# Value products of groups 3, 6, 9 and 12 in two parts, one of them with VectorE's subtraction; output products moved

## The chip, the cores and the metric

One core of a Trainium2 chip runs the whole program. The metric is the time of one execution in microseconds (us); lower is better. The five engines run their own instruction queues in order and meet at semaphores: PE (TensorE), DVE (VectorE), ACT (ScalarE), POOL (GpSimd) and SP, which here only issues DMAs.

## The reference, cut to what matters

```
x = x + xattn(layernorm(x), ctx)     # 256 rows, 16 heads of 128, 4 key/value heads, 4096 context rows
x = x + mamba2(layernorm(x))
x = x + experts(layernorm(x))        # 32 experts, top 6, and a shared one

scores = einsum('blhd,bmhd->bhlm', q, k_full) * scale + mask     # m: 4096 context rows and 256 own rows
probs  = softmax(scores, axis=-1)
out    = einsum('bhlm,bmhd->blhd', probs, v_full)
return out.reshape(B, L, nh * hd) @ wo
```

Everything is in float32. The change is in the cross attention and in the hand-over from it to the second part.

## The kernel before

The program is written out by hand, one function for each engine; the order of the calls in it is the order on the engine. About 240 us go to projecting the context, 450 us to the attention, 60 us to the second part and 230 us to the experts.

In the attention the 4352 keys of a head are 17 groups of 256 (`NG`); group 16 (`SELF`) holds the own rows and a causal mask. A counter `s` runs over the 272 groups in which scores are made, and `n = s - LEAD` (29 groups behind) over the groups whose weights meet the values. So one step of TensorE, `in_turns(score(s), weigh(n), n)`, interleaves six score matmuls for a later head with the value products of group n. All engines' loops run over the same steps:

- ScalarE copies the scores out of PSUM (`take_scores(s)`, line 1643), takes the exponential of two groups at once (`exponential`, line 1647, a "quad"), and for some groups rounds the weights to a high part (`high_of_weights`, line 1653).
- VectorE keeps the running maximum of the scores (`running_max`, lines 1093 to 1109), folds it, and subtracts the head's maximum from a quad (`subtract_max`, line 1135).
- GpSimd adds the weights of the 17 groups (`add_weights`, line 1939) and makes the low parts (`rest_of_weights`, line 1953).

A value product of a plain group is one float32 matmul for each of its two key tiles (line 641; the trace shows it as two MATMUL records). In the groups of `SPLITS` = (2, 7, 12) it is three float32r matmuls for each tile: values times high part, values times low part, low part of the values times high part (lines 635, 637, 639). The high and low parts of the weights lie in a ring of two buffers, `pT`. The low part of group n is issued on GpSimd in step n-1, the high part on ScalarE in step n-4.

The score banks are four PSUM banks in turn, so scores of group s need the maximum of group s-4 to be taken. The first head's subtractions stand `SOONER` = 4 steps ahead of the others'. `TURN_AT`, `REDUCE_AT` and `SPREAD_AT` say at which step the maxima are transposed (line 660), reduced (line 1127) and spread (line 668) for head 0, head 1, the middle heads and head 15. `sum_weights(h)` (line 675) sums a head's weights over the partitions.

The output projection needs `wo` in a high part (`wo_hi`, four loads of 1 MB, line 2155) and a low part. `project_main(0, i)` puts two float32r matmuls with the high part into step `WO_MAIN + i` = 246 + i. After the attention SP loads `w_z` for the second part, and ScalarE and VectorE split `w_xa`.

## Time and profile before

| | |
|---|---|
| median of 3 executions | 987.16 us (986.3 to 987.94) |
| profiled execution, its own time | 985.39 us |
| its span | 983.7 us |
| PE busy | 971.0 us, 99% |
| DVE busy | 769.7 us, 78% |
| ACT busy | 613.4 us, 62% |
| POOL busy | 573.8 us, 58% |
| mean granted TensorE clock | 0.998 of 2.4 GHz |

Busy shares are means over stages that differ; what a stage waits for is read in its own stretch. A busy PE may be working at half its clock.

### The profile page before, as it was taken

Reading aid. Unit: us, or ns where it says so; the run is one execution under the profiler, and the core shown is the slowest. Engines: PE = TensorE matmul, PEld = TensorE weight load, DVE = VectorE, ACT = ScalarE, POOL = GpSimd, SP = SyncE. Lnnn points to the kernel's source line nnn. Section 1 sums busy time; section 2 is a strip of 40 time slices with the busy share of each in tenths; the row PEclk is TensorE's granted clock in tenths of the full one; section 3 lists DMA queues with packets and bytes.
Section 4 is the critical chain, followed back from the end, with each engine's and each line's share of the span. In section 5 each row is a group of like instructions: output and inputs, shape, how many; then the busy total and the mean of one; then the engine's idle time right before and its main releaser. Section 6 shows DMA issues by size and latency. Waiting matters only on the chain.

```text
span 983.7 us, 15941 instructions
## 1 busy us (share of the span) xinstructions
PE 971.0 (99%) x5695; PEld 856.4 (87%) x5695; DVE 769.7 (78%) x1167; ACT 613.4 (62%) x1042; POOL 573.8 (58%) x545
## 2 busy tenths in 40 slices
PE   9999999999989999999999999989999999999998
PEld 7888888888889999999999999978789988888887
DVE  6754777654988888888898898877798877777775
ACT  5444354336757777777767767753597666666663
POOL 4754555453389999999999999993001132222222
PEclk9999999999999999999999999999999999999999
DMA  8679866679403121141105033261700785555540
GB/s 303 192 247 318 270 208 222 193 243 312 163 1 128 56 76 34 44 140 55 54 1 159 25 112 111 76 211 57 288 12 1 287 299 197 190 180 184 188 157 22
DMA packets 70926, 147.89 MB, mean 150 GB/s; under 512 B 5792, under 2 KB 50240, under 8 KB 69312
## 3 DMA queue, kind: packets, MB, share of 16 engines
q1 hardware_dynamic: 70848, 146.88, 44.1%
q8 instruction: 46, 0.75, 0.3%
q14 instruction: 32, 0.26, 0.1%
HBM read 109.60 MB, written 37.26 MB: 149 GB/s over the span
## 4 chain that ended last, share of the span: by engine, by line
PE 85%; DVE 9%; POOL 2%; DMA 1%; issue 1%; ACT 0%; SPq 0%; DVEq 0%
PE bank L641 19%; PE bank L612 17%; PE bank L520 11%; PE bank L538 11%; PE bank L941 9%; PE bank L943 5%; PE bank L749 1%; PE bank L692 1%; POOL k_rs L1908 1%; PE bank L635 1%; PE bank L637 1%; PE bank L639 1%; PE bank L547 1%; DVE turned L1071 1%; DVE bank L1109 1%
## 5 line engine op out<-in xcount | busy, mean ns | idle before, releaser
L612 PE MATMUL bank<-qT_hi,kT 128*128 128x256 f32 (+1 forms) x1088 | 295.1, 345 | 2.5 <-DVE first_max L1105 2.5
L1939 POOL TENSOR_TENSOR first_max<-first_max,weights 128x512 f32<-128x512 f32 x210 | 270.7, 1289 | 20.0
L641 PE MATMUL bank<-weights,vN 128*128 128x256 f32 (+1 forms) x896 | 259.6, 377 | 0.4 <-ACT weights L1647 0.4
L1643 ACT COPY weights<-bank 128x512 f32<-128x512 f32 (+1 forms) x272 | 154.6, 581 | 102.8 <-PE bank L612 63.4
L612 PEld LDWEIGHTS bank<-qT_hi,kT 128*128 128x128 f32 x1088 | 196.1, 189 | 21.1 <-issue 2.9
L1109 DVE TENSOR_TENSOR first_max<-bank,first_max 128x512 f32<-128x512 f32 x196 | 135.0, 689 | 34.6 <-ACT weights L1643 29.1
L1135 DVE TENSOR_TENSOR weights<-weights,bank 128x1024 f32<-128x1024 f32 x128 | 154.6, 1211 | 6.2 <-PE bank L668 6.2
L612 PE MATMUL bank<-qT_lo,kT 128*128 128x256 f32 (+1 forms) x544 | 153.5, 282 | 0.0
L1647 ACT ACTIVATE weights<-weights 128x1024 f32<-128x1024 f32 x144 | 144.0, 1003 | 9.5 <-DVE weights L1135 8.7
L641 PEld LDWEIGHTS bank<-weights,vN 128*128 128x128 f32 x896 | 142.0, 189 | 3.8 <-ACT weights L1647 0.6
L538 PE MATMUL bank<-w_ctx_hi,ctx_hl 128*128 128x512 f32 x512 | 144.4, 394 | 0.6 <-ACT w_ctx_hi L1604 0.6
L941 PE MATMUL bank<-fT_parts,e_hl 128*128 128x512 f32 x392 | 140.0, 395 | 0.0
L538 PEld LDWEIGHTS bank<-w_ctx_hi,ctx_hl 128*128 128x128 f32 x512 | 94.7, 188 | 20.1 <-ACT w_ctx_hi L1604 1.1
L943 PE MATMUL bank<-fT_parts,e_hl 128*128 128x256 f32 x392 | 110.1, 281 | 0.0
L612 PEld LDWEIGHTS bank<-qT_lo,kT 128*128 128x128 f32 x544 | 103.1, 190 | 0.0
L1781 ACT CAST e_hl<-e_raw 128x1536 fp32r<-128x1536 f32 x51 | 75.5, 1482 | 38.6 <-PE bank L520 38.1
L1998 POOL TENSOR_TENSOR hid<-hid,comb 128x256 f32<-128x256 f32 x32 | 26.3, 822 | 108.3 <-ACT hid L1836 90.8
L941 PEld LDWEIGHTS bank<-fT_parts,e_hl 128*128 128x128 f32 x392 | 73.5, 188 | 17.7 <-DVE e_hl L1354 0.4
L1551 ACT ACTIVATE k_stage<-bank,k_w 128x512 fp32r<-128x512 f32 x32 | 22.1, 690 | 103.2 <-PE bank L547 103.2
L1354 DVE TENSOR_TENSOR e_hl<-e_raw,e_hl 128x1536 fp32r<-128x1536 f32 x49 | 85.9, 1753 | 0.0
L538 PE MATMUL bank<-w_ctx_lo,ctx_hl 128*128 128x512 f32 x256 | 79.3, 391 | 0.0
L1908 POOL TENSOR_TENSOR k_rs<-k_ssq,power 128x4 f32<-128x4 f32 x32 | 32.5, 1016 | 79.9 <-DVE k_ssq L1016 79.7
(262 smaller groups left out, 1748.1 us busy)
## 6 DMA issues: line engine op xcount, KB each, us to landing
e_raw<-in_experts SPq DMA_DIRECT2D x51, 768.0 KB, 4.3
k_spill<-k_stage SPq DMA_DIRECT2D x16, 1024.0 KB, 5.8
kT<-k_spill SPq DMA_DIRECT2D x15, 1024.0 KB, 5.2
v_spill<-v_stage SPq DMA_DIRECT2D x16, 512.0 KB, 6.7
vN<-v_spill SPq DMA_DIRECT2D x16, 512.0 KB, 3.5
ctx_raw<-in_ctx SPq DMA_DIRECT2D x15, 512.0 KB, 5.1
w_raw<-in_w_qkv SPq DMA_DIRECT2D x6, 1024.0 KB, 5.5
wo_chunk<-in_wo SPq DMA_DIRECT2D x32, 128.0 KB, 3.8
```

Source lines behind the costliest of these rows:

```text
L520: done = e.matmul(dst, lhs(a), rhs(w), start=first and m == 0, stop=last and m == 2)
L538: done = e.matmul(bank[2 * j + z][:, :], ctx_hl[z][:, a, k, :], w_ctx[w][:, k, j, :], start=m < 2, stop=m >= len(order) - 2)
L612: done = e.matmul(dst, kT[:, w, kt * P:(kt + 1) * P], qT[a][:, h, q0:L], start=m == 0, stop=m == 2)
L641: done = e.matmul(dst[:, q0:L], vN[:, kt, :], weights[:, cols], start=kt == 0, stop=kt == KTILES - 1)
L941: e.matmul(bank[b][:, :].rearrange("p (x t) -> p x t", x=2), w[:, 0, m, k * P:(k + 1) * P], fT_parts[:, :, k, :], start=k == 0, stop=False)
L943: done = e.matmul(bank[b][:, 0:L], w[:, 1, m, k * P:(k + 1) * P], fT_parts[:, 0, k, :], start=False, stop=k == KD - 1)
L1109: e.tensor_tensor(top[:, :], here[:, :], top[:, :], ALU.max).then_inc(maxed, 1)
L1135: e.tensor_tensor(rows, rows, top.unsqueeze(1).to_broadcast([P, 4, L]), ALU.subtract).then_inc(subbed, 1)
L1354: e.tensor_tensor(dst[:, 1], src[:, :, :], dst[:, 0], ALU.subtract).then_inc(e_lo, 1)
L1643: e.copy(s_buf[h % 2][:, g, 0:width(g)], bank[SCORE_BANKS[s % len(SCORE_BANKS)]][:, 0:width(g)]).then_inc(taken, 1)
L1647: e.activation(quad(h, j), quad(h, j), ACT.Exp, scale=SCALE).then_inc(expd, 1)
L1939: e.tensor_tensor(run_sum[:, :], run_sum[:, :], here, ALU.add).then_inc(summed, 1)
```

## The change

- `SPLITS` becomes (3, 6, 9, 12): four of a head's 17 groups are made of float32r products in place of three. GpSimd makes the low parts of 3, 6 and 12. VectorE makes that of 9 (`BY_DVE`), in its step n = 7, ahead of the running maximum of that step. One more group of low values per key/value head is made, spilled and loaded.
- For head 0, `SOONER` is 2, and turning, reducing and spreading its maximum each stand one step later.
- `sum_weights(h)` for heads 0 to 13 stands four steps later (after group 5 of the next head instead of group 1).
- The first four output products stand at steps 243 to 246 and read `wo_first`, a buffer that SP fills long before; the others start at step 249. For that half of `w_xa` is loaded only after the attention, ahead of `w_z`.

```diff
-TURN_AT, REDUCE_AT, SPREAD_AT = (5, 5, 4, 3), (1, 5, 5, 4), (6, 7, 6, 5)
+TURN_AT, REDUCE_AT, SPREAD_AT = (6, 5, 4, 3), (2, 5, 5, 4), (7, 7, 6, 5)
-SOONER = 4
+SOONER = 2
-SPLITS = (2, 7, 12)
+SPLITS = (3, 6, 9, 12)
+BY_DVE = 9
-WO_MAIN, WO_REST = 246, 250
+WO_MAIN, WO_PAUSE, WO_REST = 243, 2, 250
...
+        wo_first = Region(nc, region["v"].base + 4 * KD * DI + 2048 + 2 * 4 * DI, 4 * 4 * DM).take("wo_first", [4, DM], F32R)
...
-                if g in SPLITS:
-                    pe.wait_ge(p_lo, split_number(n) + 1)
+                if g == BY_DVE:
+                    pe.wait_ge(p_lo_dve, NWC + h + 1)
+                elif g in SPLITS:
+                    pe.wait_ge(p_lo, pool_splits(n) + 1)
...
-                if k == 1 and h in range(H15):
+                if h in range(H15) and k == (1 if h == H15 - 1 else 5):
                     sum_weights(h)
-                if WO_MAIN <= n < WO_MAIN + H15 - 1:
-                    project_main(0, n - WO_MAIN)
+                i = n - WO_MAIN if n < WO_MAIN + 4 else max(n - WO_MAIN - WO_PAUSE, 3)
+                if i in range(4) and n < WO_MAIN + 4 or i in range(4, H15 - 1):
+                    project_main(0, i)
...
+            def rest_of_weights(n):
+                dve.wait_ge(p_hi, split_number(n) + 1)
+                wait_ring(dve, n)
+                e.tensor_tensor(ring_of(n)[:, 1], weights_of(n), ring_of(n)[:, 0], ALU.subtract).then_inc(p_lo_dve, 1)
...
                     subtract_max(h, j)
+                if (n + 2) % NG == BY_DVE and 0 <= n + 2 < NH * NG:
+                    rest_of_weights(n + 2)
                 running_max(s)
...
-                if (n + 1) % NG in SPLITS:
+                if (n + 1) % NG in SPLITS and (n + 1) % NG != BY_DVE:
                     rest_of_weights(n + 1)
...
-                e.dma_start(w_xa[:, :, :], t["w_in"][:, :, DI:2 * DI]).then_inc(w_xa_in, 16)
+                e.dma_start(w_xa[:, 0:2, :], t["w_in"][:, 0:2, DI:2 * DI]).then_inc(w_xa_in, 16)
+                e.dma_start(wo_first[:, :, :].bitcast(F32), wo_parts[0][:, 0:4]).then_inc(wo_hi_in[0], 16)
...
-            for j in range(NH // 4):
+            for j in range(1, NH // 4):
...
+            e.dma_start(w_xa[:, 2:KD, :], t["w_in"][:, 2:KD, DI:2 * DI]).then_inc(w_xa_in, 16)
             e.dma_start(w_z[:, :, :], t["w_in"][:, :, 0:DI]).then_inc(w_z_in, 16)
```

ScalarE in a middle head, steps 2 to 6 before: COPY is a score copy, ACTIVATE an exponential, CAST a high part; the copy of 384 is the SELF group of the later head.

```order
L1647 ACTIVATE weights1_122<-weights1_122 128x1024 [waits subbed]
L1643 COPY weights0_121<-bank6 128x512 [waits summed,pv,scored]
L1653 CAST pT0_126<-weights1_122 128x512 [waits expd]
L1643 COPY weights0_121<-bank0 128x384 [waits summed,pv,maxed]
L1647 ACTIVATE weights1_122<-weights1_122 128x1024 [waits subbed]
L1643 COPY weights1_122<-bank2 128x512 [waits summed,pv,scored]
L1643 COPY weights1_122<-bank6 128x512 [waits pv,scored]
L1647 ACTIVATE weights1_122<-weights1_122 128x1024 [waits subbed]
```

The same steps of the change:

```order
L1665 ACTIVATE weights1_122<-weights1_122 128x1024 [waits subbed]
L1671 CAST pT1_127<-weights1_122 128x512 [waits pv,expd]
L1661 COPY weights0_121<-bank7 128x512 [waits summed,pv,scored]
L1661 COPY weights0_121<-bank0 128x384 [waits summed,pv,maxed]
L1665 ACTIVATE weights1_122<-weights1_122 128x1024 [waits subbed]
L1661 COPY weights1_122<-bank2 128x512 [waits summed,pv,scored]
L1671 CAST pT0_126<-weights1_122 128x512 [waits pv,expd]
L1661 COPY weights1_122<-bank6 128x512 [waits scored]
L1665 ACTIVATE weights1_122<-weights1_122 128x1024 [waits subbed]
```

The high part that stood behind the copy of group 15's scores (step 3) stands ahead of it (group 6's, step 2), and a second one, group 9's, stands between the score copies of groups 0 and 1 of the head after.

VectorE in a middle head, the same steps and the one after, in the change: L1120 and L1116 are running maxima, L1146 a subtraction of the maximum, L1104, L1107 and L1132 the SELF group's mask, maxima and fold.

```order
L1120 TENSOR_TENSOR first_max_123<-bank2,first_max_123 128x512 [waits maxed,taken]
L1146 TENSOR_TENSOR weights1_122<-weights1_122,bank3 128x1024
L1104 TENSOR_TENSOR bank6<-bank6,causal_53 128x384 [waits scored]
L1107 TENSOR_TENSOR first_max_123<-bank6,first_max_123 128x256 [waits maxed]
L1107 TENSOR_TENSOR first_max_123<-bank6,first_max_123 128x128 [waits maxed]
L1132 TENSOR_REDUCE both_max_132<-first_max_123 128x256 [waits maxed]
L1146 TENSOR_TENSOR weights1_122<-weights1_122,bank3 128x1024
L1116 TENSOR_TENSOR first_max_123<-bank0,weights1_122 128x512 [waits maxed,taken]
L1174 TENSOR_TENSOR pT0_126<-weights1_122,pT0_126 128x512 [waits pv,p_hi]
L1120 TENSOR_TENSOR first_max_123<-bank2,first_max_123 128x512 [waits maxed,taken]
```

Before, the same rows stand there without L1174. It stands behind the maximum of group 1 of the later head (L1116), which waits for ScalarE's copy of those scores.

## Rows read from the trace of the kernel before

**Rows 1.** Busy time of each engine in two stretches (TensorE's clock third from the end).

```profile
594.00:621.00 27.00, 27.00 (x184) 25.41 (x183) 23.73 (x34) 19.34 (x30) 25.51 (x23) 1.00 0.14 57
655.00:660.00 5.00, 5.00 (x18) 4.02 (x17) 0.90 (x2) 0.41 (x1) 4.85 (x4) 0.66 0.24 97
```

**Rows 2.** Timeline of PE in a middle head: start, duration, instruction.

```profile
600.94 0.38 PE L660 MATMUL bank<-ident,both_max 128*128 128x128 f32 x2
...
615.20 0.59 PE L675 MATMUL bank<-both_sum,ones 128*128 128x256 f32 x2
615.44 0.47 PE L612 MATMUL bank<-qT_hi,kT 128*128 128x256 f32 x1
...
621.57 0.59 PE L612 MATMUL bank<-qT_hi,kT 128*128 128x256 f32 x2
...
623.15 0.47 PE L612 MATMUL bank<-qT_hi,kT 128*128 128x256 f32 x1
...
626.13 0.59 PE L612 MATMUL bank<-qT_hi,kT 128*128 128x256 f32 x2
...
627.90 0.38 PE L660 MATMUL bank<-ident,both_max 128*128 128x128 f32 x2
```

**Rows 3.** Timeline of ACT in the same head.

```profile
617.61 1.06 ACT L1647 ACTIVATE weights<-weights 128x1024 f32<-128x1024 f32 x1
618.57 0.58 ACT L1643 COPY weights<-bank 128x512 f32<-128x512 f32 x1
...
623.63 1.07 ACT L1643 COPY weights<-bank 128x512 f32<-128x512 f32 x2
...
627.67 0.62 ACT L1653 CAST pT<-weights 128x512 fp32r<-128x512 f32 x1
628.19 0.58 ACT L1643 COPY weights<-bank 128x512 f32<-128x512 f32 x1
```

**Rows 4.** Timeline of DVE in the same head; in brackets its idle time and who ended it.

```profile
619.19 0.69 DVE L1109 TENSOR_TENSOR first_max<-bank,first_max 128x512 f32<-128x512 f32 x1 [0.75 <-ACT weights L1643]
...
624.73 0.69 DVE L1105 TENSOR_TENSOR first_max<-bank,weights 128x512 f32<-128x512 f32 x1 [0.60 <-ACT weights L1643]
```

**Rows 5.** Timeline of POOL, in the same head and in the last but one.

```profile
621.10 1.29 POOL L1953 TENSOR_TENSOR pT<-weights,pT 128x512 fp32r<-128x512 f32 x1
622.35 6.89 POOL L1939 TENSOR_TENSOR first_max<-first_max,weights 128x512 f32<-128x512 f32 x5
...
657.31 6.87 POOL L1939 TENSOR_TENSOR first_max<-first_max,weights 128x512 f32<-128x512 f32 x5
```

**Rows 6.** Timeline of DVE, two sums of one form in the last head.

```profile
675.49 0.69 DVE L1152 TENSOR_TENSOR own_sum<-own_sum,weights 128x512 f32<-128x512 f32 x1
...
679.75 1.23 DVE L1152 TENSOR_TENSOR own_sum<-own_sum,weights 128x512 f32<-128x512 f32 x1
```

**Rows 7.** Timeline of POOL beside the second of them.

```profile
679.14 1.30 POOL L1953 TENSOR_TENSOR pT<-weights,pT 128x512 fp32r<-128x512 f32 x1 [4.30 <-ACT pT L1653]
```

**Rows 8.** Timeline of DVE where the first head's values meet the third head's scores.

```profile
276.48 0.69 DVE L1105 TENSOR_TENSOR first_max<-bank,weights 128x512 f32<-128x512 f32 x1
```

**Rows 9.** Timeline of PE: there, in the last but one head, and behind the attention.

```profile
277.31 0.47 PE L612 MATMUL bank<-qT_hi,kT 128*128 128x256 f32 x2 [2.48 <-DVE first_max L1105]
...
654.50 0.85 PE L692 MATMUL bank<-wo_hi,outT 128*128 128x512 f32 x2 [2.40 <-DMA wo_hi<-wo_parts]
...
670.96 0.81 PE L692 MATMUL bank<-wo_hi,outT 128*128 128x512 f32 x2
...
701.27 3.60 PE L749 MATMUL bank<-w_z,uT 128*128 128x512 f32 x8
```

**Rows 10.** DMA issues from 560 to 760 us: KB each, median us to landing.

```profile
wo_hi<-wo_parts SPq DMA_DIRECT2D x4, 1024.0 KB, 5.2
...
w_z<-in_w_in SPq DMA_DIRECT2D x1, 2048.0 KB, 7.7
```

**Rows 11.** Timeline of SP behind the attention.

```profile
691.65 0.55 SPq L2158 DMA_DIRECT2D w_z<-in_w_in  x1
```

More of the change, by code:

```diff
@@ L150, in split_number, with pool_splits @@
     return sum(1 for m in range(n) if m % NG in SPLITS)
+def pool_splits(n):
+    return sum(1 for m in range(n) if m % NG in SPLITS and m % NG != BY_DVE)
 def split_tiles(i):
@@ L271, in build_program @@
         own_sum = Region(nc, region["k"].base + 4 * NH * DM, 4 * GW).take("own_sum", [GW])
-        own_both = pt_.take("own_both", [L])
+        own_both = sp_.take("own_both", [L])
         pT = [pt_.take(f"pT{i}", [2, GW], F32R) for i in range(RING)]
@@ L393, in build_program @@
         pv, summed, sum_all, ho, oT_hi, oT_lo = (sem(n) for n in ("pv", "summed", "sum_all", "ho", "oT_hi", "oT_lo"))
-        wo_hi_done, wo_lo_done, wo_done, x1 = sem("wo_hi"), sem("wo_lo"), sem("wo_done"), sem("x1")
+        wo_hi_done = p_lo_dve = sem("wo_hi_then_p_lo_dve")
+        wo_lo_done, wo_done, x1 = sem("wo_lo"), sem("wo_done"), sem("x1")
         wx_hi_done, wx_lo_done, uT_hi, uT_lo, tap = (sem(n) for n in ("wx_hi", "wx_lo", "uT_hi", "uT_lo", "tap"))
@@ L691, in project_main @@
                 for a in range(2):
-                    e.matmul(bank[tt][:, :], outT[a][:, h, tt * P:(tt + 1) * P], wo_hi[:, h, :], start=i == 0 and a == 0, stop=False)
+                    e.matmul(bank[tt][:, :], outT[a][:, h, tt * P:(tt + 1) * P], wo_first[:, h, :] if h < 4 else wo_hi[:, h, :], start=i == 0 and a == 0, stop=False)
             def project_rest(tt, i):
@@ L1682, in act_program @@
             for n in range(len(PAIRS)):
-                act.wait_ge(*(w_xa_in, chunks_in + 16) if n else (w_xb_in, chunks_in + 32))
+                act.wait_ge(*(w_xa_in, chunks_in + 32) if n else (w_xb_in, chunks_in + 32))
                 e.copy(pair_weights(n, 0), pair_weights(n, None)).then_inc(wx_hi_done, 1)
```

## The prediction

> **What bounds the kernel now.** I read the windows first. In the attention PE is busy for all of 27.00 us of a stretch, at the full clock (1.00, its 2.4 GHz level), and POOL for 25.51 of 27 [rows 1]. So PE sets the time there, and POOL stands close behind it. Next the timeline of PE, for the length of its steps. A step with a plain group lasts 1.58 us (621.57 to 623.15); the split group and the plain one behind it last 2.98 us together (623.15 to 626.13), where two plain ones would last 3.16. A head lasts 26.96 us (600.94 to 627.90), and the sum of the weights takes 0.24 to 0.25 us (615.20 to 615.44) [rows 2]. A split group is thus worth 0.16 to 0.18 us of PE; I take 0.16, since the step behind such a group gains a part that others could lose. Third I looked for PE's idle time. There is 2.48 us at 277.31, when PE waits for VectorE's maximum L1105, and 2.40 us at 654.50, when it waits for the first quarter of `wo_hi` [rows 9]. Behind the second the granted clock falls to 0.66 in the mean of 5 us, which is the 1.2 GHz level for about 3.4 of them [rows 1], so the wait costs some 1.7 us more.
>
> **PE's gain.** One more split group in each of 16 heads is worth 16 x 0.16 = 2.6 us, if its low part is there in time.
>
> **Is it there in time?** This is the step that decides, so I follow one middle head from the start of its step 2, and call that moment 0 (615.44 before). ScalarE's exponential of that step starts at 617.61, the copy of group 15's scores at 618.57 [rows 3]. The changed order puts group 6's high part between the two. A high part that depends on the exponential starts 0.03 us behind its end, and the next copy 0.52 behind the high part's start (627.67, 628.19) [rows 3]. Step 2 is no longer a split group, and its scores are done 0.15 sooner, so the exponential starts at 2.02, the high part at 3.11, ready at 3.73, and the copy at 3.63 in place of 3.13: 0.5 later. VectorE's maximum of group 15 waited for that copy (0.75 us idle, 619.19), and from there VectorE works without a break through the subtraction, the mask and the SELF group's maxima, on which ScalarE's next copy hangs. All of it moves 0.5 later. Then the new high part of group 9 stands between the copies of the later head's groups 0 and 1, and costs 0.52 again. VectorE's L1105 waits for the second copy (0.60 us idle, 624.73) [rows 4]. It stood at 9.29; it will stand at 9.29 + 0.50 + 0.52 = 10.3. The low part of group 9 stands right behind it, at 10.3 + 0.6 = 10.9 (VectorE issues the next independent instruction about 0.6 us after the start of one of 0.69).
>
> PE comes to group 9 as follows: steps 2, 4, 5, 7 and 8 plain, 3 and 6 split, which with the shorter SELF step is 10.69 (626.13 less 615.44; before, too, two of these seven were split) [rows 2], plus 0.25 for the sum of the weights, which now stands behind step 5, plus 0.30 for the first score product: 11.24.
>
> If the subtraction takes 0.69 us, as the maxima of that size do, it ends at 11.6, and PE waits 0.4 us. But it reads both its inputs from SBUF, while the maxima and subtractions around it read one from PSUM. What that means shows in two sums of one form: 0.69 us alone, and 1.23 us when GpSimd was at work from 679.14 to 680.44 [rows 6, 7]. It began at 679.75 and ended at 680.98, which is 0.54 us behind GpSimd's end. VectorE stood still until GpSimd's instruction was over.
>
> The Trainium skill states this as a rule that speaks against the change: "SBUF — State Buffer", section "Who interferes with whom", has it that a VectorE instruction with two SBUF inputs contends with a GpSimd instruction that reads SBUF, and that the second to be issued is blocked for the whole of the first. By that rule the sum is that of the forecast, without it that of the second rival below; the 1.23 us go with the rule.
>
> So where is GpSimd then? Its low part of group 6 needs the high part, ready at 3.73, and starts at about 3.8; its own chain would let it start earlier, since it has no more to do in a head than now and PE's step gets longer. A low part holds it for 1.25 us (621.10 to 622.35), each addition for 1.37 (five in 6.84, of 1.29 busy) [rows 5]. Additions 5 to 9 follow, and the fifth runs from 3.8 + 1.25 + 4 x 1.37 = 10.5 to 11.8. VectorE comes at 10.9, in the middle of it, and ends at 11.8 + 0.54 = 12.3. PE goes on at 12.35, after a wait of 1.1 us.
>
> The cost for one middle head is 1.1 - 0.16 = 0.95 us. Bounds: a wait of 0 if VectorE comes before GpSimd's addition does (at 10.4, 0.5 us sooner than I reckon), 0.4 us if it is not blocked, and 1.6 us if it comes right behind the start of one. This chain exists in the heads whose steps also score a SELF group and the group 1 behind it, which are heads 0 to 13. For heads 1 to 13: 13 x 0.95 = **+12.4 us**, with ends of -2.1 and +18.7.
>
> **Head 0.** VectorE is the late one here: PE waited 2.48 us for L1105, which ends at 277.17 [rows 8, 9]. In the change the reduction stands behind one more maximum, which saves VectorE a wait of 0.5 us, and the last two subtractions stand behind L1105 (0.5 us). So L1105 comes about 1 us sooner, less up to 0.5 for the mask, which also reads SBUF twice. But then PE no longer waits at step 10 for the maximum but at step 9 for the low part, which stands behind L1105 and the two subtractions: 276.2 + 0.5 + 0.7 = 277.3, or 277.9 behind a GpSimd addition. A whole split step of 1.4 us has to follow before PE is where it was at 277.31. Sum: **+1.4 to +2.0, taken as +1.8**, of which the sum of the weights that now comes later in head 1 gives back 0.25 until the tail. The waits of PE at steps 3 and 6 for low parts that come later, for the subtractions of head 0 start 1 us later, end inside this one.
>
> **The end of the attention.** The 2.40 us wait for `wo_hi` and the 1.7 us at half clock go [rows 1, 9]: 4.1. The other three quarters then become late. The last is issued behind GpSimd's addition of group 15 in head 14, which ends at 657.31 + 6.87 = 664.2 before [rows 5] and some 0.8 sooner against PE in the change; 5.2 us to landing [rows 10] gives 668.6. PE would want it at about 666. The product of step 256 stood at 670.96 [rows 9], and one more is behind PE by then, 0.46 us. That is 2.4 + 0.5, so **-2.9 us**, with ends of -4.1 and -1, as the later quarters wait for nothing or as they wait longer. The last head has one split group more, -0.15.
>
> **Behind the attention.** `w_z`, issued at 691.65 [rows 11], landed 7.7 us later with 2 MB [rows 10], so at 699.4, and PE begins its product at 701.3 [rows 9]: 1.9 us in hand. Now 1 MB of `w_xa` stands ahead of it, and one more MB costs 7.7 - 5.2 = 2.5 us [rows 10]. **+0.6**, with ends of 0 and +2. The further low values in the context stage (two VectorE instructions of 0.69 us with an input in PSUM, a spill) and four loads of 128 KB I take as hidden behind PE, since the same work for three groups shows in none of the rows as a wait; without that cover it is 2 x 0.69 = 1.4 us.
>
> **Sum.** Taken without rounding the parts, -0.25 included: +12.4 + 1.8 - 0.25 - 2.9 - 0.15 + 0.6 = **+11.5 us**. On the profiled execution's own time, 985.4, this gives 996.9. The median of the runs is 1.8 us higher, 987.2, and so is what I forecast: 998.6.
>
> **The rivals.**
> - *The low part comes in time (faster).* If ScalarE's chain is 0.5 us shorter than I reckon, VectorE comes between two of GpSimd's additions, at or before 10.4, and PE does not wait at step 9 of the middle heads. For it: VectorE idles 3.3 of 27 us, 0.60 of them right ahead of L1105 [rows 1, 4]. Against it: both high parts stand ahead of that place in ScalarE's queue. 13 x -0.16 = -2.1, so -2.1 + 1.55 - 2.9 - 0.15 + 0.6 = -3.0: 984.2. The sign turns at a wait of 0.23 us for one head (13 x 0.07 = 0.9, the rest of the sum).
> - *GpSimd does not block VectorE.* The wait is 0.4: 13 x 0.24 = 3.1, head 0 is at +1.4, and 3.1 + 1.4 - 0.25 - 2.9 - 0.15 + 0.6 = +1.8: 989.0. Against it stands the sum of 1.23 us.
> - *More than forecast.* GpSimd falls behind by the 0.3 us a head that VectorE takes from it, or PE's clock falls after a wait as it did at 655. 1.4 us for each head and more: above 1002.
>
> **How the numbers follow.** The measurement of this kernel can't tell changes under 0.2%, 2 us, from none. The forecast case has 0.56, more than forecast 0.06, no blocking 0.16 (0.10 the same, 0.06 slower, since its price lies just under the bound), the low part in time 0.22. This gives slower 0.68, same 0.10, faster 0.22. The forecast case alone spans 994 to 1002. The range reaches down to the low part in time and up to the top of the forecast case: 984 to 1001.5.
>
> **What would show it.** In the changed kernel's trace, PE waits 1.1 us for the new VectorE line in step 9 of each of heads 1 to 13, and a head lasts 27.9 us in place of 26.96. That line lasts 1.2 to 1.5 us, not 0.69, and ends 0.54 behind the end of an addition of GpSimd. L1105's successor starts 1.0 later against PE's step 2. In head 0 the 2.48 us wait is gone, and one of about 2.5 stands one step earlier. Between 649 and 672 us the waits are for the later quarters of `wo_hi`, the first product waits for nothing, and the clock stays at 2.4 GHz. `w_z` lands 2 to 3 us later after its place in the queue. I am wrong if PE's head is shorter than 26.96 us; then either the new line ends before 11.2, or the copies of ScalarE do not stand where I put them.

## The result, and the profile of the changed kernel

The changed kernel takes 1001.58 us (median of four executions, 999.66 to 1003.53), the kernel before 986.73 us (median of four, 985.55 to 987.94). The ratio is 1.0153, with a 95% interval from 1.014 to 1.0166: slower by 14.9 us. The forecast was 998.6 us, slower, with a range up to 1001.5. The direction and the main place of the loss were right. The size was not: the measured loss is 3.4 us above the 11.5 us of the sum, and the time lies above the range (by 0.08 us).

The profiled execution of the changed kernel took 1003.53 us (span 1001.8), that of before 985.39. So these two traces stand 18.1 us apart, not 14.9; 1.8 of them lie ahead of the attention, and the paragraph on the start, below, takes them up.

The windows of the changed kernel, for one middle head and for the first head behind its longest wait (TensorE's granted clock is third from the end):

```profile
594.00:622.00 28.00, 27.07 (x186) 25.36 (x185) 24.95 (x34) 20.07 (x32) 25.95 (x23) 1.00 0.46 152
277.00:280.00 3.00, 0.38 (x2) 0.39 (x3) 3.00 (x6) 0.49 (x1) 2.78 (x3) 0.83 0.00 0
280.00:283.00 3.00, 3.00 (x15) 3.00 (x15) 1.08 (x3) 0.84 (x2) 3.00 (x3) 0.50 0.01 3
283.00:286.00 3.00, 3.00 (x12) 2.53 (x12) 0.68 (x2) 1.71 (x3) 2.71 (x3) 0.53 0.00 0
```

In the middle head PE is now idle for 0.9 us, where it was never idle before [rows 1]. In the first head it ran at half clock for most of 280 to 286.

The timeline of PE in the middle head, which answers to [rows 2] (its step 2 begins at 605.40):

```profile
605.40 0.58 PE L620 MATMUL bank<-qT_hi,kT 128*128 128x256 f32 x2
...
611.70 0.59 PE L685 MATMUL bank<-both_sum,ones 128*128 128x256 f32 x2
...
616.51 0.47 PE L620 MATMUL bank<-qT_hi,kT 128*128 128x256 f32 x1
617.91 0.39 PE L645 MATMUL bank<-pT,vN 128*128 128x256 f32 x1 [0.93 <-DVE pT L1174]
...
619.31 0.38 PE L670 MATMUL bank<-ident,both_max 128*128 128x128 f32 x2
...
647.23 0.38 PE L670 MATMUL bank<-ident,both_max 128*128 128x128 f32 x2
```

The product with group 9's high part should stand 0.31 us behind the score product at 616.51, as it does in a split step without a wait; it stands 1.40 behind it. PE is thus held up by 1.09 us, of which the bracket shows 0.93 as idle. A head lasts 27.92 us (619.31 to 647.23).

The timelines of ACT, DVE and POOL in that head, which answer to [rows 3], [rows 4] and [rows 5]:

```profile
607.40 1.07 ACT L1665 ACTIVATE weights<-weights 128x1024 f32<-128x1024 f32 x1
608.50 0.62 ACT L1671 CAST pT<-weights 128x512 fp32r<-128x512 f32 x1
...
614.55 0.63 ACT L1671 CAST pT<-weights 128x512 fp32r<-128x512 f32 x1
615.07 0.60 ACT L1661 COPY weights<-bank 128x512 f32<-128x512 f32 x1
```

```profile
615.70 0.69 DVE L1116 TENSOR_TENSOR first_max<-bank,weights 128x512 f32<-128x512 f32 x1 [1.11 <-ACT weights L1661]
616.30 1.55 DVE L1174 TENSOR_TENSOR pT<-weights,pT 128x512 fp32r<-128x512 f32 x1
617.77 0.68 DVE L1120 TENSOR_TENSOR first_max<-bank,first_max 128x512 f32<-128x512 f32 x1
```

```profile
609.20 1.28 POOL L1971 TENSOR_TENSOR pT<-weights,pT 128x512 fp32r<-128x512 f32 x1 [0.23 <-ACT pT L1671]
610.43 8.58 POOL L1957 TENSOR_TENSOR first_max<-first_max,weights 128x512 f32<-128x512 f32 x6
```

The fifth and the sixth of those six additions by themselves:

```profile
616.02 1.28 POOL L1957 TENSOR_TENSOR first_max<-first_max,weights 128x512 f32<-128x512 f32 x1
617.44 1.57 POOL L1957 TENSOR_TENSOR first_max<-first_max,weights 128x512 f32<-128x512 f32 x1
```

Counted from 605.40, the exponential starts at 2.00 (forecast 2.02), group 6's high part at 3.10 (3.11), its low part on GpSimd at 3.80 (3.8), VectorE's maximum at 10.30 (10.3) and the new low part at 10.90 (10.9). It ends at 12.45 (12.3) and PE goes on at 12.51 (12.35). The low part lasts 1.55 us, where the forecast had 1.4 for a blocked one and 0.69 for an unblocked one. It is issued while the fifth addition runs (616.02 to 617.30) and ends 0.55 us behind it. The sixth, issued while the low part runs, lasts 1.57 us in place of 1.28: GpSimd loses 0.3 us.

The timeline of PE elsewhere, which answers to [rows 9]: the start of the scores, the first head, the third head's transpose, the later quarters of `wo_hi`, and the product with `w_z`.

```profile
237.26 0.48 PE L620 MATMUL bank<-qT_hi,kT 128*128 128x256 f32 x2
...
266.78 0.39 PE L645 MATMUL bank<-pT,vN 128*128 128x256 f32 x1 [1.33 <-POOL pT L1971]
...
279.62 0.58 PE L645 MATMUL bank<-pT,vN 128*128 128x256 f32 x1 [2.72 <-DVE pT L1174]
...
311.81 0.38 PE L670 MATMUL bank<-ident,both_max 128*128 128x128 f32 x2
...
682.37 0.73 PE L702 MATMUL bank<-wo_hi,outT 128*128 128x512 f32 x2 [0.54 <-DMA wo_hi<-wo_parts]
...
717.19 0.40 PE L708 MATMUL bank<-wo_lo,outT 128*128 128x512 f32 x1
719.42 1.10 PE L760 MATMUL bank<-w_z,uT 128*128 128x512 f32 x2 [1.83 <-issue]
```

The same three places in the kernel before: the start of the scores, the third head's transpose, the last output product ahead of `w_z`.

```profile
235.50 0.48 PE L612 MATMUL bank<-qT_hi,kT 128*128 128x256 f32 x2
...
304.31 0.38 PE L660 MATMUL bank<-ident,both_max 128*128 128x128 f32 x2
...
701.03 0.40 PE L698 MATMUL bank<-wo_lo,outT 128*128 128x512 f32 x1
```

Where the two traces part, read from these rows and [rows 2, 9]: 1.76 us at the start of the scores, 7.50 at the third head's transpose, 19.33 at the fifteenth's (627.90 and 647.23), 16.16 at the last output product, 18.15 at the product with `w_z`. Behind that nothing changes.

The table has the same distances for all kernels of this study, in us, each read from its trace: when the scores start, from there to the third head's transpose, the mean head from there to the fifteenth's, from there to the first product with `w_z`, and PE's wait ahead of that product. Beside the median, each row is one execution. The kernels are described in the next section; the repeat of the changed kernel is experiment 9, and experiment 7 is missing because its trace is of an execution that was 2.5 times as long.

| kernel | median | scores start | to third head | a head | to `w_z` | its wait |
|---|---|---|---|---|---|---|
| before | 986.7 | 235.50 | 68.81 | 26.97 | 73.37 | 0 |
| changed | 1001.6 | 237.26 | 74.55 | 27.95 | 72.19 | 1.83 |
| changed, again (9) | 1001.8 | 237.70 | 73.36 | 27.94 | 72.25 | 1.90 |
| 1 low part sooner | 992.0 | 237.06 | 69.31 | 27.31 | 74.33 | 1.67 |
| 2 short addition | 991.7 | 236.88 | 72.77 | 27.13 | 71.43 | 1.54 |
| 3 GpSimd makes all | 1002.8 | 237.15 | 69.29 | 28.10 | 75.15 | 1.48 |
| 4 three groups | 985.2 | 236.80 | 68.22 | 27.00 | 72.27 | 0.34 |
| 5 filled wait | 999.5 | 236.90 | 71.75 | 27.95 | 71.52 | 0.32 |
| 6 first head as before | 1003.4 | 236.55 | 75.57 | 27.95 | 72.09 | 1.54 |
| 8 three groups, halves | 984.5 | 235.41 | 68.23 | 26.99 | 72.30 | 0 |
| 10 `w_z` in halves | 998.2 | 237.25 | 73.35 | 27.96 | 70.29 | 0 |
| 11 the end alone | 985.3 | 235.93 | 68.77 | 26.97 | 71.50 | 0.52 |
| 12 sooner and short | 983.3 | 235.72 | 69.33 | 26.76 | 72.38 | 1.93 |

### The profile page after: what moved, and what is told of

Same layout as the page of the kernel before. It is cut to its first block, busy times and chain, and to the rows that moved or that the text cites. A ratio compares the mean times of both kernels' runs of the same rounds, so it can differ in the third digit from the quotient of the medians.

```text
span 1001.8 us, 16079 instructions
## 1 busy us (share of the span) xinstructions
PE 973.8 (97%) x5727; PEld 856.2 (85%) x5727; DVE 789.4 (79%) x1185; ACT 624.0 (62%) x1058; POOL 579.9 (58%) x545
## 4 chain that ended last, share of the span: by engine, by line
PE 68%; POOL 11%; DVE 9%; ACT 5%; issue 4%; DMA 2%; SPq 0%; POOLq 0%; DVEq 0%
PE bank L620 12%; PE bank L528 11%; PE bank L651 11%; PE bank L546 9%; PE bank L952 9%; POOL first_max L1957 7%; PE bank L954 5%; POOL pT L1971 2%; DVE pT L1174 2%; ACT weights L1661 2%; PE bank L760 1%; ACT weights L1665 1%; ACT pT L1671 1%; POOL k_rs L1926 1%; PE bank L645 1%
## 5 line engine op out<-in xcount | busy, mean ns | idle before, releaser
L1957 POOL TENSOR_TENSOR first_max<-first_max,weights 128x512 f32<-128x512 f32 x210 | 274.5, 1307 | 18.8
L651 PE MATMUL bank<-weights,vN 128*128 128x256 f32 (+1 forms) x832 | 240.7, 376 | 0.0
L1146 DVE TENSOR_TENSOR weights<-weights,bank 128x1024 f32<-128x1024 f32 x128 | 154.6, 1211 | 2.3 <-PE bank L678 2.3
L1120 DVE TENSOR_TENSOR first_max<-bank,first_max 128x512 f32<-128x512 f32 x196 | 134.5, 686 | 27.2 <-ACT weights L1661 22.6
L651 PEld LDWEIGHTS bank<-weights,vN 128*128 128x128 f32 x832 | 131.2, 189 | 2.5
L528 PE MATMUL bank<-e_hl,act 128*128 128x512 f32 x306 | 78.8, 394 | 0.0
```

The costliest lines, as they stand in the source:

```text
L528: done = e.matmul(dst, lhs(a), rhs(w), start=first and m == 0, stop=last and m == 2)
L651: done = e.matmul(dst[:, q0:L], vN[:, kt, :], weights[:, cols], start=kt == 0, stop=kt == KTILES - 1)
L1120: e.tensor_tensor(top[:, :], here[:, :], top[:, :], ALU.max).then_inc(maxed, 1)
L1146: e.tensor_tensor(rows, rows, top.unsqueeze(1).to_broadcast([P, 4, L]), ALU.subtract).then_inc(subbed, 1)
L1957: e.tensor_tensor(run_sum[:, :], run_sum[:, :], here, ALU.add).then_inc(summed, 1)
```

## The experiments

All are edits of the changed kernel. Times are medians; the ratio is to the kernel before on the same chip.

### 1. Group 9's parts one step sooner

ScalarE makes group 9's high part right behind the exponential, and VectorE its low part ahead of the maximum of group 1, where it was idle for 1.11 us.

```diff
-                if (n + EXP_AHEAD) % NG in SPLITS and 0 <= n + EXP_AHEAD < NH * NG:
-                    high_of_weights(n + EXP_AHEAD)
+                m = n + EXP_AHEAD + ((n + EXP_AHEAD + 1) % NG == BY_DVE)
+                if m % NG in SPLITS and (m > n + EXP_AHEAD or m % NG != BY_DVE) and 0 <= m < NH * NG:
+                    high_of_weights(m)
...
-                if (n + 2) % NG == BY_DVE and 0 <= n + 2 < NH * NG:
-                    rest_of_weights(n + 2)
+                if (n + 3) % NG == BY_DVE and 0 <= n + 3 < NH * NG:
+                    rest_of_weights(n + 3)
```

> The changed kernel, with ScalarE's high part of group 9 one step sooner (right behind the exponential, ahead of group 0's score copy) and VectorE's low part one step sooner (ahead of the maximum of group 1, in VectorE's idle 1.1 us). Theory (the wait is nothing but this low part coming late behind a GpSimd addition): the low part may still last about 1.6 us, since it is still beside an addition, but it ends at least 0.3 us ahead of PE's need, the 0.93 us wait in heads 1 to 13 is gone, a head lasts 26.8 us and the time falls by 13 x 1.1 = 14 us, to 986 to 988. Rival A (VectorE itself has become too slow by 1.55 us a head, wherever this work stands): the following maximum is late by the same amount, PE waits for a score bank instead, and a head stays above 27.5. Rival B (ScalarE): group 0's copy is 0.5 us later and PE waits for it.

Measured: 992.04 us (991.8 to 992.55), ratio 1.0057 (1.0042 to 1.0072). The wait for group 9 is gone in heads 1 to 13 (head 0 keeps one of 1.51 us at 278.22), and 9.5 us with it, but not the 14 that were expected. The third and fourth head last 26.77 and 26.78 us. Then PE meets a wait of 0.22 us for GpSimd's low part (364.02), and from there a head lasts 27.4 us (the first of them 27.6). The timelines of POOL and DVE in this kernel:

```profile
599.39 1.28 POOL L1972 TENSOR_TENSOR pT<-weights,pT 128x512 fp32r<-128x512 f32 x1
600.62 8.64 POOL L1958 TENSOR_TENSOR first_max<-first_max,weights 128x512 f32<-128x512 f32 x6
609.21 1.29 POOL L1972 TENSOR_TENSOR pT<-weights,pT 128x512 fp32r<-128x512 f32 x1
610.45 6.89 POOL L1958 TENSOR_TENSOR first_max<-first_max,weights 128x512 f32<-128x512 f32 x5
```

```profile
603.07 0.82 DVE L1174 TENSOR_TENSOR pT<-weights,pT 128x512 fp32r<-128x512 f32 x1 [0.29 <-ACT pT L1671]
```

No row of POOL has an idle time in brackets: it works without a break, and its six additions beside the low part take 8.64 us, where five take 6.89 (1.38 each, so six would take 8.3). So the bound seems to have passed to GpSimd; experiment 12 tests it. None of the rivals on record had that; the theory that the wait was the only loss does not hold.

### 2. A short addition beside the low part

```diff
+                    w = 4 if g == BY_DVE else 2 * L
-                    e.tensor_tensor(run_sum[:, :], run_sum[:, :], here, ALU.add).then_inc(summed, 1)
+                    e.tensor_tensor(run_sum[:, 0:w], run_sum[:, 0:w], here[:, 0:w], ALU.add).then_inc(summed, 1)
```

> The changed kernel, but GpSimd's addition of group 9's weights covers 4 of 512 columns, so that the long addition beside VectorE's low part is nearly gone (the sum of the weights is left incomplete). Theory (the low part is blocked by that addition): it lasts 0.7 us in place of 1.53, starts where it did, PE is held up by 0.2 us in place of 1.1, a head lasts 27.0 us, and the time is 1001.6 - 13 x 0.9 = 990. Rival (the instruction is slow by itself, with its two SBUF inputs and its rounded output): it stays at 1.5 us and the time at 1001.6.

Measured: 991.73 us (990.4 to 993.06), ratio 1.0053 (1.0037 to 1.007). The timelines of DVE and of PE in this kernel:

```profile
605.33 0.69 DVE L1116 TENSOR_TENSOR first_max<-bank,weights 128x512 f32<-128x512 f32 x1 [1.12 <-ACT weights L1661]
605.94 0.68 DVE L1174 TENSOR_TENSOR pT<-weights,pT 128x512 fp32r<-128x512 f32 x1
```

```profile
606.13 0.47 PE L620 MATMUL bank<-qT_hi,kT 128*128 128x256 f32 x1
606.68 0.38 PE L645 MATMUL bank<-pT,vN 128*128 128x256 f32 x1
```

And the short addition itself, on POOL:

```profile
606.09 0.60 POOL L1958 TENSOR_TENSOR first_max<-first_max,weights 128x4 f32<-128x4 f32 x1
```

VectorE's low part is issued 0.61 us behind the maximum, as in the changed kernel (0.60), and lasts 0.68 in place of 1.55. PE's product stands 0.55 behind its score product, so PE is held up by 0.24 us in place of 1.09. Nothing but GpSimd's work has changed, so the blocking by GpSimd's addition is shown. It goes the other way too: the addition of 4 columns, issued while the low part runs, lasts 0.60 us and ends 0.07 behind it, where in experiment 12 it lasts 0.20 us away from the low part. Both traces agree with the rule of the Trainium skill ("SBUF — State Buffer", section "Who interferes with whom") on which the forecast leaned.

### 3. GpSimd makes all four low parts

```diff
-BY_DVE = 9
+BY_DVE = -1
```

> The changed kernel, with GpSimd making all four low parts (VectorE none). GpSimd is busy for 25.5 of 27 us with three of them, and one is 1.25 us more: 26.8 us a head. Theory: GpSimd just keeps up, PE waits 0 to 0.4 us a head, a head lasts 26.8 to 27.2, and the time is 987 to 993. Rival (GpSimd, which also loses time to VectorE, falls behind): PE waits 0.5 us or more in each head for a low part or for the sum, and the time is 996 or more.

Measured: 1002.81 us (1002.18 to 1005.04), ratio 1.0171 (1.0151 to 1.019). The rival is right, though the wait is 0.45 us where it had 0.5 or more. The timeline of POOL, and PE's wait that comes once in every head:

```profile
584.74 1.27 POOL L1971 TENSOR_TENSOR pT<-weights,pT 128x512 fp32r<-128x512 f32 x1
585.98 4.08 POOL L1957 TENSOR_TENSOR first_max<-first_max,weights 128x512 f32<-128x512 f32 x3
590.01 1.28 POOL L1971 TENSOR_TENSOR pT<-weights,pT 128x512 fp32r<-128x512 f32 x1
591.25 6.87 POOL L1957 TENSOR_TENSOR first_max<-first_max,weights 128x512 f32<-128x512 f32 x5
```

```profile
614.14 0.38 PE L645 MATMUL bank<-pT,vN 128*128 128x256 f32 x1 [0.45 <-POOL pT L1971]
```

A head lasts 28.10 us, and POOL again has no idle time. So GpSimd needs 28.10 us with four low parts, which is 28.10 - 1.25 = 26.85 with three, next to 26.97 us of a head before. [rows 1] show it busy for 25.51 of 27; the rest is the gaps between its instructions (five additions span 6.87 to 6.89 us [rows 5] and are busy for 1.29 each), and POOL uses them in no trace. In experiment 1 it needed 27.4, so VectorE's low part takes about 0.5 us from it. The 0.3 by which one addition is stretched are part of that; no row shows where the rest lies.

### 4. Groups 3, 6 and 12 alone

```diff
-SPLITS = (3, 6, 9, 12)
-BY_DVE = 9
+SPLITS = (3, 6, 12)
+BY_DVE = -1
```

> The changed kernel, with groups 3, 6 and 12 in parts and 9 plain. It keeps the moved output products, the split load of w_xa, and the first head's later subtractions. Theory (the loss sits in group 9): heads 1 to 13 last 26.96 as in the kernel before; the end of the attention gains 2.9 us, w_z loses 2.0; in the first head PE's clock stays at 1.00 and it costs no more than before. Time 986. Rival (the first head's loss of about 4.7 us comes from its later subtractions, not from group 9): the first head still costs 3 to 4 us more than before, and the time is 989 to 991.

Measured: 985.21 us (984.19 to 986.85, ten executions), ratio 0.9984 (0.9975 to 0.9994). The theory's 986 is nearly met, and the rival's 989 to 991 is out: with the later subtractions and without group 9 the stretch to the third head takes 68.22 us, 0.59 less than before. So the loss hangs on group 9. The rest of the change is worth a gain of one to two microseconds (the ratio gives 0.6 to 2.5).

### 5. PE's wait of the first head filled

```diff
+                for _ in range(16 if n == BY_DVE else 0):
+                    e.matmul(bank[TURN_BANK][:, 0:L], kT[:, 0, 0:P], qT[0][:, 0, 0:L], start=True, stop=True)
                 in_turns(score(s), weigh(n), n)
```

> The changed kernel with 16 float32r matmuls of 256 columns, whose result nobody reads, put into PE's 2.72 us wait of the first head (ahead of step 9; about 1.9 us of work that ends before the low part comes). Theory (some 3 us of the first head's loss are the granted clock, which reads 0.50 for about 6 us behind that wait): the clock stays at 1.00 there, the third head's transpose comes about 2.9 us sooner after the start of the scores, and the time is 998.7. Rival (the clock falls because of the whole stretch before, with its 1.33 and 0.47 us waits, or its cost is hidden by VectorE, which is late anyway): nothing is gained and the time stays at 1001.6.

Measured: 999.46 us (999.27 to 1001.32), ratio 1.0128 (1.011 to 1.0145). The windows and the timeline of PE in this kernel:

```profile
280.00:283.00 3.00, 3.00 (x24) 2.84 (x23) 1.65 (x3) 2.20 (x4) 2.91 (x3) 1.00 0.01 3
283.00:286.00 3.00, 3.00 (x25) 2.89 (x24) 0.81 (x3) 1.24 (x3) 2.72 (x3) 1.00 0.02 5
```

```profile
279.32 0.39 PE L645 MATMUL bank<-pT,vN 128*128 128x256 f32 x1 [0.89 <-DVE pT L1176]
```

PE still goes on only when the low part is there, and the 1.33 and 0.46 us waits ahead of it are as they were, but the clock stays at 1.00. The stretch to the third head is 71.75 us, where the changed kernel took 74.55 and 73.36 in its two traces. So the half clock costs 1.6 to 2.8 us there, and what is left of the first head's loss is 71.75 - 68.81 - 0.98 (the second head's wait lies in the stretch too) = 1.96 us. The median is 2.1 us under the changed kernel's first, and 2.4 under its second. The theory holds, with less than the 2.9 us that it had.

### 6. The first head's constants as before

```diff
-TURN_AT, REDUCE_AT, SPREAD_AT = (6, 5, 4, 3), (2, 5, 5, 4), (7, 7, 6, 5)
-SOONER = 2
+TURN_AT, REDUCE_AT, SPREAD_AT = (5, 5, 4, 3), (1, 5, 5, 4), (6, 7, 6, 5)
+SOONER = 4
```

> The changed kernel, with the first head's four constants as before (subtractions 4 steps sooner in place of 2, the turning, reducing and spreading one step sooner). Theory (the first head's loss is group 9's low part, which stands behind the maximum that was late before): the waits of 1.33 and 0.47 us at groups 3 and 6 go, PE waits 3 to 4 us at group 9, the clock falls behind it, and the time is 1001 to 1003. Rival (the later subtractions make it): the clock stays at 1.00, the first head costs 25.6 us again, and the time is 997.

Measured: 1003.42 us (1002.24 to 1004.61), ratio 1.0164 (1.0146 to 1.0181). The wait at group 9, and the windows from there:

```profile
280.58 0.58 PE L645 MATMUL bank<-pT,vN 128*128 128x256 f32 x1 [5.33 <-DVE pT L1174]
```

```profile
280.00:283.00 3.00, 2.42 (x11) 2.42 (x12) 1.82 (x3) 0.00 (x0) 2.86 (x2) 0.50 0.01 3
283.00:286.00 3.00, 3.00 (x15) 2.72 (x15) 0.69 (x1) 2.08 (x4) 2.62 (x3) 0.59 0.00 0
```

The wait is longer than I had put it (5.33 us, not 3 to 4), group 3's shrinks from 1.33 to 0.96 and does not go, group 6's stays (0.48), and the stretch takes 75.57 us. In these traces the first head is thus 1 to 2 us dearer without the later subtractions; in the times it does not show, for the ratio's interval overlaps that of the changed kernel in experiment 9. The rival is out.

### 7 and 10. `w_z` in two halves

PE's product waits for the first half, and for the second only at its third quarter. The first half counts on a semaphore that is free by then.

```diff
-                pe.wait_ge(w_z_in, 32 * NWC + 16)
+                pe.wait_ge(w_raw_in, 16 * NW + 16)
...
+                    if k == 2:
+                        pe.wait_ge(w_z_in, 32 * NWC + 16)
...
-            e.dma_start(w_z[:, :, :], t["w_in"][:, :, 0:DI]).then_inc(w_z_in, 16)
+            e.dma_start(w_z[:, 0:2, :], t["w_in"][:, 0:2, 0:DI]).then_inc(w_raw_in, 16)
+            e.dma_start(w_z[:, 2:KD, :], t["w_in"][:, 2:KD, 0:DI]).then_inc(w_z_in, 16)
```

> The changed kernel, with w_z loaded in two halves of 1 MB, and PE's product waiting for the second only at its third quarter. Theory (PE waits 1.83 us because w_z is 2 MB behind 1 MB of w_xa): the first half lands about 2.5 us sooner, PE waits 0 to 0.2 us for it, and reaches the second half when it lands; 1.8 us are gained, and the time is 999.8. Rival (PE waits for ScalarE's copy of the transposed rows, which is behind four casts of w_xa): the wait stays at 1.83, and the time at 1001.6.

Measured: 998.65 us (median of three executions, 998.51 to 998.84), ratio 1.0115 (1.0098 to 1.0133). The profiled execution was a fourth one of 2506 us, in which PE's own products take more than twice as long, so its waits say nothing of the others. The kernel was taken once more:

> The changed kernel with w_z in two halves once more, for its trace and for a comparison on one chip. If PE's wait is for w_z's landing, the wait of 1.8 us is gone in the trace and the time is 1.8 us under that of the changed kernel; if it is ScalarE's copy, both stay.

Measured: 998.21 us (997.14 to 1000.58), ratio 1.0123 (1.0106 to 1.014), beside 1.0157 for the changed kernel on the same chip. The timeline of PE:

```profile
716.16 0.40 PE L708 MATMUL bank<-wo_lo,outT 128*128 128x512 f32 x1
716.39 3.74 PE L762 MATMUL bank<-w_z,uT 128*128 128x512 f32 x8
```

The product starts 0.23 us behind the last output product, without a wait. The way from the fifteenth transpose is 1.96 us shorter than in experiment 9. So PE waited for the landing of `w_z`, not for ScalarE. The medians differ by 3.6 us, the two profiled executions by 2.1. The other 1.6 are in no trace, but the record has a hint: three of this kernel's four executions have a mean granted clock of 1.000 (997.14 to 998.39 us) and the profiled one has 0.998 (1000.58 us), where all four of experiment 9 have 0.998. So most of the 1.6 us may be time at half clock; in which wait it was saved is not shown.

### 8. Three groups and `w_z` in halves

> Groups 3, 6 and 12 in parts, 9 plain, and w_z in two halves: the version with both faults mended. Groups 3, 6 and 12 alone gave 985.2. If the wait for w_z of about 2 us is there too and is gone, 983.4; if the wait is ScalarE's, 985.2.

Measured: 984.47 us (983.83 to 985.24, ten executions), ratio 0.9971 (0.9961 to 0.998). This is the version that beats both kernels, by 3 us over the one before. Over experiment 4 the gain is not shown: the intervals of the two ratios overlap, and the wait for `w_z` was only 0.34 us there. In its trace that wait is gone, and one of 1.79 us for the second quarter of `wo_hi` (657.30) is there as in experiment 4, which had 1.76. The windows of this kernel, then of experiment 4:

```profile
660.00:665.00 5.00, 5.00 (x20) 4.14 (x20) 0.99 (x1) 1.87 (x3) 4.70 (x5) 0.83 0.62 210
```

```profile
660.00:665.00 5.00, 5.00 (x25) 3.97 (x23) 2.56 (x3) 3.42 (x5) 4.56 (x5) 1.00 0.61 210
```

Behind waits of the same length the clock fell in one execution and not in the other. At 0.83, the half clock holds for 1.7 of these 5 us and costs 0.85.

### 9. The changed kernel again

> The changed kernel itself, beside the next three on one chip. It should give 1001.6 (ratio 1.015), with the clock at 0.50 behind the first head's wait of 2.7 us, 27.95 us a head and a wait of 1.8 us for w_z.

Measured: 1001.84 us (1001.33 to 1002.68), ratio 1.0157 (1.0142 to 1.0172). The wait of the first head is 2.75 us. Behind it the clock is 0.74 and 0.69:

```profile
280.00:283.00 3.00, 2.91 (x17) 2.75 (x17) 2.02 (x4) 1.42 (x2) 3.00 (x3) 0.74 0.01 3
283.00:286.00 3.00, 3.00 (x16) 2.65 (x15) 0.90 (x2) 1.13 (x3) 2.78 (x3) 0.69 0.00 0
```

That is less time at half clock than the first trace showed behind a wait of the same length, and the stretch to the third head is 1.2 us shorter.

### 11. The end of the attention alone

```diff
-SPLITS = (3, 6, 9, 12)
-BY_DVE = 9
+SPLITS = (2, 7, 12)
+BY_DVE = -1
...
-                if h in range(H15) and k == (1 if h == H15 - 1 else 5):
+                if h in range(H15) and k == 1:
```

and the first head's constants as in experiment 6.

> The kernel before with only the end of the attention changed: groups 2, 7 and 12 in parts, the first head's constants and the sum of the weights as before, but the first four output products at steps 243 to 246 from their own buffer and half of w_xa loaded behind the attention. The forecast had -2.9 for the end of the attention and +0.6 for w_z; the changed kernel showed -3.1 and +2.0. By the forecast's sizes the time is 2.3 us under that of before (984.9), by the measured ones 1.1 us under it (986.1).

Measured: 985.27 us (983.34 to 986.64, ten executions), ratio 0.9985 (0.9975 to 0.9994), so 1.5 us less than before (0.6 to 2.5), between the two expectations. PE waits 0.52 us for `w_z`, which landed 9.7 us behind its issue. From the fifteenth transpose to the product with `w_z` it takes 71.50 us, 1.87 less than before.

### 12. The low part sooner, with the short addition

> The version with group 9's high and low parts one step sooner, and GpSimd's addition of group 9 cut to 4 of 512 columns (the sum of the weights is left incomplete). That version with the whole addition gave 26.78 us for heads 1 and 2 and 27.38 to 27.42 for the later ones, in which GpSimd never stood idle. Theory (GpSimd has become the bound there): with 1.37 us less work in a head GpSimd keeps up, every head lasts 26.8 us, and the time is 992.0 - 11 x 0.6 = 985.4 or a little less. Rival (it is VectorE's or ScalarE's new place that PE meets from head 3 on): the heads stay at 27.4 and the time at 992.

Measured: 983.30 us (982.81 to 984.63), ratio 0.9968 (0.9957 to 0.998). Every head lasts 26.76 us. The timeline of POOL:

```profile
592.73 7.52 POOL L1959 TENSOR_TENSOR first_max<-first_max,weights 128x512 f32<-128x512 f32 x6
600.70 1.28 POOL L1973 TENSOR_TENSOR pT<-weights,pT 128x512 fp32r<-128x512 f32 x1 [0.45 <-ACT pT L1671]
```

GpSimd now waits for ScalarE. Its six additions take 7.52 us in place of the 8.64 of experiment 1. With that 1.1 us less for it, PE sets the time again, and four split groups give 0.21 us a head over three. So the bound of experiment 1 was GpSimd. This kernel leaves work out and is no version to use.

## Why the prediction came out as it did

**The middle heads: right.** The step "PE goes on at 12.35, after a wait of 1.1 us" measured 12.51 and 1.09. Heads 1 to 13 cost 0.98 us each, 12.8 us, against +12.4. Both causes are shown: the place by experiment 1, the blocking by experiment 2. The three middle rows of the forecast (10.3, 10.9, 3.8) were met to 0.01 us; each came from differences between rows of the trace before. That the wait came out so close is in part luck: PE came at 11.42, not at 11.24, and the low part ended at 12.45, not at 12.3, and these two misses cancel.

**Head 0: the step that failed.** The first head is the term that was mis-sized most. The step was "Sum: +1.4 to +2.0, taken as +1.8". It counted the waits at the full clock. At the full clock it was right: experiment 5 gives 1.96. But the clock fell to its 1.2 GHz level behind the 2.72 us wait, and the term came to 3.6 us (experiment 9) and 4.8 (the first trace). I had seen such a fall behind the 2.40 us wait for `wo_hi` and counted it there, but gave it here only to the rival "more than forecast", because the 2.48 us wait at 277.31 [rows 9] had no fall behind it: the kernel before has a clock of 1.00 from 278 to 288 in its trace. That was one execution. Of the 41 others of the kernel before, taken beside the experiments, 18 have a mean granted clock of 0.998, like the traced one, with a median of 985.9 us; 22 have 0.996 or 0.997, with a median of 987.7, and one 0.995. So in more than half of them the clock was down for longer than in the trace that I read; behind which wait is not shown.

**`w_z`: the second term that was too small, at the end of its bounds.** The step "+0.6, with ends of 0 and +2" measured 2.0 us in both traces of the changed kernel. The load landed 11.0 us behind its issue, where I had 7.7 + 2.5 = 10.2, and the issue itself came 0.43 us later behind that of `w_xa`, which I had left out. The landing varies: experiments 4, 5 and 11 show 9.5 to 9.7 us and waits of 0.32 to 0.52, the other edits with one load of `w_z`, and the changed kernel, 10.7 to 11.2. Why is open.

**The sum of the weights of head 0.** The -0.25 was wrong. The sum is moved within the same stretch between two transposes, and nothing was gained.

**The end of the attention: right.** Forecast -2.9 and -0.15; measured 16.16 - 19.33 = -3.17. The first product waits for nothing, and PE waits 0.54 and 0.31 us for later quarters, with the clock at 1.00. A wait of 0.45 us for the low part in head 14 (672.40), which the forecast did not have, lies in it too.

**The start: a term put at nothing.** The context stage, which I took as hidden, ended 1.76 us later in the first trace. In it PE waits 1.52 us at 8.80 for ScalarE's high part of the context's weights (0.64 before) and 0.47 us at 225.01 for that of the context (0 before). The first of these varies whatever the groups: 1.19 us in experiment 4, with three, and 0.51 in experiment 12, with four. The second is above 0.3 us in five of the nine traces with four groups and in none of the four with three, and the scores start at 235.41 to 236.80 us with three groups and at 235.72 to 237.70 with four, a mean of 235.9 against 236.9. So a cost of about 1 us for the fourth group's low values, near the 1.4 that the forecast named for work that is not hidden, is not excluded and not shown.

Together, from the trace of experiment 9: 12.6 + 3.6 - 3.2 + 2.1 = 15.1 us, and 2.2 at the start give the 17.3 us between its span and that of the kernel before. The medians are 14.9 us apart, near the sum without the start. But that is no proof that they hold nothing of it: the traced execution of the kernel before is 1.3 us under its median, and by its clock one of the quicker ones. The forecast had 11.5.

**The rival "the low part comes in time" was priced wrong.** It was given 984.2 us. Experiment 1 is that case, and gives 992.0. The failed step is "its own chain would let it start earlier, since it has no more to do in a head than now": GpSimd needs 26.85 us a head with three low parts, and about 0.5 more when VectorE's low part runs beside it. I had read 25.51 us busy as 1.5 us of room. With the low part in time, but GpSimd making three others and all the additions, the fourth group still does not pay: 27.4 us a head against 26.97. Other places for the low part were not tried; one that takes more than 0.1 us from GpSimd could not pay either.

## What to carry to other kernels

A subtraction with both inputs in SBUF, given to VectorE beside a GpSimd that hardly rests, costs both of them: here 0.9 us on VectorE (1.55 against 0.68) and about 0.5 on GpSimd (experiment 1). Before work is moved to an engine or around one, find the time that each engine needs for the period with its gaps, not its busy time; an engine at 25.5 of 27 us had 0.1 us to give. And where a change makes one long wait for PE, the price has two parts, the wait and the clock behind it; work that nobody needs, put into the wait, kept the clock up here. And read the clock of more than one execution before a fall of it is put at nothing.

## What the runs showed of the hardware

- The length of a wait does not tell whether the clock falls. It did not behind 2.48 us in the kernel before and 1.76 us (experiment 4), it did behind 1.79 (8), 2.40, 2.72 and 2.75 us. Behind one and the same wait, that for `w_z`, it stayed at 1.00 after 1.90 us (experiment 9, 718 to 723) and read 0.66 in 5 us after 1.93 us (experiment 12, 698 to 703). And the same kernel had 0.50 and 0.53 in two windows of 3 us in one execution and 0.74 and 0.69 in another.
- Three of the terms above vary by 1 to 2 us between traces whose edits do not touch them: the start of the scores (235.41 to 236.80 us with three groups), the landing of `w_z` (9.5 us in experiment 5, 11.0 in the changed kernel) and the cost of the half clock (1.6 and 2.8 us in two executions of the changed kernel). So one trace of each kernel can part by more than the medians (18.1 us here, against 14.9).
- Of two such instructions on SBUF, the one issued second was held up: VectorE's low part, issued inside GpSimd's addition, ended 0.55 us behind it, and GpSimd's addition of 4 columns, issued inside VectorE's low part, took 0.60 us in place of 0.20.
- One of the 72 executions of the changed kernel and its variants took 2506 us. In its trace the plain value products of 256 columns last 827 ns in the mean (380 in the changed kernel), beside a granted clock of 1.00, while an exponential on ScalarE and an addition on GpSimd last as long as ever (1.06 and 1.28 us). Its cause is open.
